# A second transposed copy of x for layer 0's residual, and a relu in two halves of PSUM banks, in a two-layer pre-activation convolution

## What is computed

```python
def _gn(v, G=8, eps=1e-5):
    # per image and group of 2 channels: (v - mean) / sqrt(var + eps)
def _conv(inputs, u, v, w, b):
    kern = jnp.einsum('lj,lk,li->ijkl', u, w, v)      # 3x3, 16 -> 16 channels
    out = lax.conv_general_dilated(inputs, kern, window_strides=(1, 1), padding='SAME', ...)
    return jax.nn.relu(out + b)
x = x + _conv(_gn(x), u0, v0, w0, b0)
x = x + _conv(_gn(x), u1, v1, w1, b1)
```

## Time and profile before

| what | value |
|---|---|
| three runs | 4683.33, 4687.26, 4693.34 us; median 4687.26 |
| the profiled execution | 4676.86 us |
| its span, first to last instruction | 4675.1 us |
| granted TensorE clock | 0.997 of full speed |
| instructions | 288889 |
| DMA | 555.71 MB, mean 119 GB/s |

### The profile page before, as it was taken

How to read it: one execution, slowest core, us unless ns; L and a number is a source line. 1 busy time by engine, 2 the same in 40 slices (tenths; PEclk the granted TensorE clock), 3 DMA queues, 4 the chain that set the end, 5 groups by cost and what they waited for, 6 DMA issues and landing times.

```text
span 4675.1 us, 288889 instructions
## 1 busy us (share of the span) xinstructions
PE 4587.9 (98%) x138240; PEld 2626.0 (56%) x138240; DVE 2845.1 (61%) x3341; ACT 2199.5 (47%) x2242; POOL 1265.0 (27%) x1093
## 2 busy tenths in 40 slices
PE   5999999999999999999999999999999999999999
PEld 3555555555555555555555555555555555555555
DVE  4656656566566566665666656656656666566564
ACT  4454444544445444444454444444544444445442
POOL 3322322323223222232232322322313223223230
PEclk9999999999999999999999999999999999999999
DMA  3333333333333333333333333333333333333323
GB/s 120 108 120 117 124 121 122 118 122 116 122 121 120 118 119 120 123 118 121 122 119 121 121 120 121 120 121 122 120 121 121 120 125 117 121 122 120 121 91 102
DMA packets 542278, 555.71 MB, mean 119 GB/s; under 512 B 16432, under 2 KB 541104, under 8 KB 541104
## 3 DMA queue, kind: packets, MB, share of 16 engines
q1 hardware_dynamic: 541104, 537.22, 35.0%
HBM read 268.72 MB, written 268.44 MB: 115 GB/s over the span
## 4 chain that ended last, share of the span: by engine, by line
PE 94%; issue 3%; ACT 1%; DVE 0%; ACTq 0%; DVEq 0%
PE ps_y L374 35%; PE ps_y L336 34%; PE ps_x L399 12%; PE ps_x L354 10%; PE ps_y L319 2%; PE ps_x L299 1%; ACT relu L457 1%; ACT relu L454 0%; PE ps_x L309 0%; DVE evens L554 0%; DVE result L571 0%; ACTq L452 0%; DVE pixels L586 0%; DVEq L100 0%; ACT evens L465 0%
## 5 line engine op out<-in xcount | busy, mean ns | idle before, releaser
L374 PE MATMUL ps_y<-odds,scaled 32*32 32x512 f32 x49152 | 1766.8, 600 | 7.9 <-issue 2.2
L336 PE MATMUL ps_y<-evens,scaled 32*32 32x512 f32 x49152 | 1745.3, 598 | 23.6 <-ACT evens L465 8.3
L574 DVE TENSOR_TENSOR odds<-ps_x,relu 128x2048 f32<-128x2048 f32 x256 | 586.8, 2292 | 1110.7 <-PE ps_x L354 842.1
L374 PEld LDWEIGHTS ps_y<-odds,scaled 32*32 32x32 f32 x49152 | 808.0, 103 | 794.2 <-issue 376.4
L336 PEld LDWEIGHTS ps_y<-evens,scaled 32*32 32x32 f32 x49152 | 852.8, 103 | 699.8 <-issue 214.0
L457 ACT ACTIVATE relu<-ps_y,bias 128x2048 f32<-128x2048 f32 x256 | 503.8, 1968 | 1094.3 <-PE ps_y L374 942.7
L280 POOL TENSOR_TENSOR fold<-fold,evens 128x1024 f32<-128x1024 f32 x384 | 845.0, 2200 | 597.3 <-DVE evens L561 309.8
L571 DVE TENSOR_TENSOR result<-ps_x,relu 128x2048 f32<-128x2048 f32 x256 | 586.6, 2292 | 636.4 <-PE ps_x L399 439.2
L454 ACT ACTIVATE relu<-ps_y,bias 128x2048 f32<-128x2048 f32 x256 | 503.7, 1968 | 920.8 <-PE ps_y L336 910.6
L354 PE MATMUL ps_x<-evens,constants 32*32 32x512 f32 x16384 | 786.7, 596 | 0.0
L399 PE MATMUL ps_x<-odds,constants 32*32 32x512 f32 x16384 | 776.2, 604 | 0.0
(11 more groups left out here) (49 smaller groups left out, 1266.7 us busy)
## 6 DMA issues: line engine op xcount, KB each, us to landing
out<-pixels SPq DMA_DIRECT2D x512, 512.0 KB, 3.5
raw<-in_x SPq DMA_DIRECT2D x256, 512.0 KB, 3.9
raw<-in_x SPq DMA_DIRECT2D x128, 576.0 KB, 4.1
raw<-in_x SPq DMA_DIRECT2D x128, 448.0 KB, 3.5
parameters<-in_params SPq DMA_DIRECT2D x2, 96.5 KB, 2.0
constants<-in_consts SPq DMA_DIRECT2D x1, 81.0 KB, 2.0
```

Source lines behind the costliest of these rows:

```text
L336: done = nc.tensor.matmul(ps_y[part, r, :], w0[rows, t * Q:(t + 1) * Q], N0[rows, k:k + EACH, i:i + HQ], start=(t == 0), stop=(t == NTAP - ...
L374: done = nc.tensor.matmul(ps_y[Q * r:Q * (r + 1), q, :], w1[p % 2][Q * q:Q * (q + 1), t * Q:(t + 1) * Q], t1[Q * q:Q * (q + 1), k:k + EACH ...
L574: nc.vector.tensor_tensor(T1[p % 2][:, EACH * f:EACH * (f + 1), 1:1 + H].rearrange("p k (r h) -> p r k h", h=HQ), ps_x[:].rearrange("p r ( ...
```

## The change

- VectorE turns x a second time, from `raw` into a new tile `N0_shifted`, one column on, that is in the pairs of `T1`. It does so in eight chunks (`turn_shifted(p, f, a)`) of the next image per image. Per image there are also three small copies into `joint`, for the pairs that cross a boundary, and one transpose of it. `SHIFTS_IN_0` and `SHIFTS_IN_1` say behind which round the chunks stand in the queue.
- The residual of layer 0 is then one product a tile with a block `same` that keeps every channel.
- The relu is two instructions of two banks each (`RELUS` = 2), in both layers. The first tap's products (`LEAD` = 1) go in the order of these halves, each half waiting for its own relu. The taps after it go over all banks in turn.
- `pixels` has four parts, used in turn, and `raw` has its own region per quarter with the column before it. SP's loads and stores stand at other places of the rounds, and a load also waits until the chunk has been turned the second time.

```diff
+RAW_Q = SLOTS * Q + ROUNDS * C
+PIXELS = 4
+SHIFTED = HALVES * ROUNDS + 4
+SHIFTS_IN_0 = (((0, 0), (0, 1)), ((1, 0),), ((1, 1),), ((2, 0),))
+SHIFTS_IN_1 = (((2, 1),), ((3, 0),), ((3, 1),), ())
...
+RELUS = 2
+BANKS = QUADS // RELUS
 HOOK_AFTER = 2
+LEAD = 1
...
+def tile_order():
+
+    lead = [(t, bank, other) for i in range(RELUS) for t in range(LEAD)
+            for other, bank in itertools.product(range(QUADS), range(BANKS * i, BANKS * (i + 1)))]
+    rest = [(t, bank, other) for t in range(LEAD, NTAP)
+            for other, bank in itertools.product(range(QUADS), range(QUADS))]
+    return lead + rest
...
+                    sp.wait_ge(shifted, shifted_by(p - 1, f, a))
...
+                ahead = C if f else 0
+                part = slice(Q * freed(f).start - ahead, Q * freed(f).stop)
+                start = raw_at(f) + C - ahead
+                sp.dma_start(raw[:, a, :, start:start + part.stop - part.start],
...
+                             pixels[:, (HALVES * f + a) % PIXELS, :].rearrange("p (q y) -> p q y", q=QUADS)
...
+                    n = round_of(0, p, 0)
+                    begun(n)
+                    load(p + 1, 3, 0)
+                    half_way(n)
+                    store(p - 2, 2, 1)
+                    begun(n + 1)
+                    load(p + 1, 3, 1)
+                    half_way(n + 1)
+                    store(p - 2, 3, 0)
...
+                    n = round_of(1, p - 1, 0)
+                    begun(n)
+                    load(p + 2, 1, 0)
+                    begun(n + 1)
+                    load(p + 2, 1, 1)
+                    half_way(n + 1)
+                    store(p - 1, 0, 0)
+                    begun(n + 2)
+                    store(p - 1, 0, 1)
...
             def conv0(p, f):
                 n = round_of(0, p, f)
-                if n:
-                    pe.wait_ge(relued, n)
...
-                for t in range(NTAP):
+                for t, r, q in tile_order():
+                    if t == 0 and q == 0 and r % BANKS == 0 and n:
+                        pe.wait_ge(relued, RELUS * (n - 1) + r // BANKS + 1)
...
+                    k = SLOTS * q + EACH * f + side
+                    rows, part = slice(Q * r, Q * (r + 1)), slice(Q * q, Q * (q + 1))
+                    done = nc.tensor.matmul(ps_y[part, r, :], w0[rows, t * Q:(t + 1) * Q],
+                                            N0[rows, k:k + EACH, i:i + HQ], start=(t == 0),
+                                            stop=(t == NTAP - 1), skip_group_check=True)
+                    last = r == QUADS - 1 and q == QUADS - 1
+                    if last and f == 0 and t == LEAD - 1:
+                        for tap in range(LEAD):
+                            wrap_pair(tap)
+                    if last and f == 0 and LEAD <= t < TAPS + 1:
...
+                    if last and t == HOOK_AFTER and f == 0:
...
-                for side in range(SIDES):
-                    for q in range(QUADS):
-                        for r in range(QUADS):
-                            k = SLOTS * q + EACH * f + side
-                            done = nc.tensor.matmul(ps_x[Q * q:Q * (q + 1), r, :], perm[Q * r:Q * (r + 1), side, :],
-                                                    N0[Q * r:Q * (r + 1), k:k + EACH, 1:1 + HQ],
-                                                    start=(side == 0), stop=(side == SIDES - 1))
+                    pe.wait_ge(shifted, SHIFTED * (p + 1))
+                for q in range(QUADS):
+                    for r in range(QUADS):
+                        done = nc.tensor.matmul(ps_x[Q * q:Q * (q + 1), r, :], same[Q * r:Q * (r + 1), :],
+                                                N0_shifted[Q * r:Q * (r + 1), q, EACH * f:EACH * (f + 1), :],
+                                                start=True, stop=True)
                 done.then_inc(x_filled, 1)
...
             def conv1(p, f):
                 n = round_of(1, p, f)
                 t1 = T1[p % 2]
-                pe.wait_ge(relued, n)
...
-                for t in range(NTAP):
+                for t, q, r in tile_order():
+                    if t == 0 and r == 0 and q % BANKS == 0:
+                        pe.wait_ge(relued, RELUS * (n - 1) + q // BANKS + 1)
...
+                    k = EACH * f + side
+                    done = nc.tensor.matmul(ps_y[Q * r:Q * (r + 1), q, :],
+                                            w1[p % 2][Q * q:Q * (q + 1), t * Q:(t + 1) * Q],
+                                            t1[Q * q:Q * (q + 1), k:k + EACH, HQ * r + i:HQ * (r + 1) + i],
+                                            start=(t == 0), stop=(t == NTAP - 1))
...
-                if y == 0:
-                    ins = nc.scalar.activation(R[:], ps_y[:], ACT.Relu, bias=bias[:, 0:1],
-                                               accum_out=acc_relu[:, f:f + 1])
-                else:
-                    ins = nc.scalar.activation(R[:], ps_y[:], ACT.Relu, bias=bias[:, 1:2])
-                ins.then_inc(relued, 1)
+                for i in range(RELUS):
+                    banks = slice(BANKS * i, BANKS * (i + 1))
+                    if y == 0:
+                        at = RELUS * f + i
+                        nc.scalar.activation(R[:, banks, :], ps_y[:, banks, :], ACT.Relu, bias=bias[:, 0:1],
+                                             accum_out=acc_relu[:, at:at + 1]).then_inc(relued, 1)
+                    else:
+                        nc.scalar.activation(R[:, banks, :], ps_y[:, banks, :], ACT.Relu,
+                                             bias=bias[:, 1:2]).then_inc(relued, 1)
...
+            def turn_shifted(p, f, a):
+                if p >= IMAGES:
+                    return
+                if p and f == 0 and a == 0:
+                    dve.wait_ge(shifted, SHIFTED * p)
+                if f == 0 and a == 0:
+                    nc.vector.tensor_copy(joint[:, :, :, C:2 * C], raw[:, :, :, C:2 * C]).then_inc(shifted, 1)
+                if p:
+                    dve.wait_ge(x_filled, round_of(0, p - 1, f) + 1)
+                turned = N0_shifted[:].rearrange("p q k (g a) -> p a q k g", a=HALVES)
+                pairs = slice(max(freed(f).start, 1), freed(f).stop)
+                start = raw_at(f) + Q * (pairs.start - freed(f).start)
+                nc.vector.transpose(turned[:, a, :, pairs, :],
+                                    raw[:, a, :, start:start + Q * (pairs.stop - pairs.start)].rearrange(
+                                        "p q (k x) -> p q k x", x=Q)).then_inc(shifted, 1)
+                if f == ROUNDS - 1 and a == 0:
+                    nc.vector.tensor_copy(joint[:, :, 1:QUADS, 0:C],
+                                          raw[:, :, 0:QUADS - 1, RAW_Q - C:RAW_Q]).then_inc(shifted, 1)
+                    nc.vector.tensor_copy(joint[:, :, 0, 0:C],
+                                          raw[:, :, QUADS - 1, RAW_Q - C:RAW_Q]).then_inc(shifted, 1)
+                if f == ROUNDS - 1 and a == 1:
+                    dve.wait_ge(shifted, SHIFTED * (p + 1) - 1)
+                    nc.vector.transpose(turned[:, :, :, 0, :], joint[:]).then_inc(shifted, 1)
+
...
-                dve.wait_ge(relued, n + 1)
+                dve.wait_ge(relued, RELUS * (n + 1))
...
+                    if ROUNDS * p + f >= PIXELS // HALVES:
+                        dve.wait_ge(image_out[a], 16 * (ROUNDS * p + f + 1 - PIXELS // HALVES))
+                    to = pixels[:, (HALVES * f + a) % PIXELS, :].rearrange("p (q k x) -> p q k x", q=QUADS, x=Q)
+                    nc.vector.transpose(to,
                                         result[:, a, :, :].rearrange("p (q k) g -> p q k g", q=QUADS)
                                         ).then_inc(turned_out, 1)
...
+            for f in range(ROUNDS):
+                for a in range(HALVES):
+                    turn_shifted(0, f, a)
...
                             turn_in(p + 1, f)
+                        for chunk in SHIFTS_IN_0[f]:
+                            turn_shifted(p + 1, *chunk)
...
                         scale_weights(0, p + 1)
                     if p:
                         turn_out(p - 1, f)
+                    for chunk in SHIFTS_IN_1[f]:
+                        turn_shifted(p + 1, *chunk)
```

More of the change, by code:

```diff
@@ L1 @@
+import itertools
 from contextlib import ExitStack
@@ L53, in turned_by, with raw_at, shifted_by @@
     return TURNS * p + (TURNS if f == ROUNDS - 1 else HALVES * (f + 1) + 1)
+def raw_at(f):
+    return Q * freed(f).start + C * f
+def shifted_by(p, f, a):
+    within = {(0, 0): 2, (3, 0): SHIFTED - 2, (3, 1): SHIFTED - 1}.get((f, a), HALVES * f + a + 2)
+    return SHIFTED * p + within
 def round_of(y, p, f):
@@ L110, in build @@
         T2 = sb("result", [P, QUADS, EACH, HQ])
-        pixels = sb("pixels", [P, HALVES, ROW])
+        pixels = sb("pixels", [P, PIXELS, QUADS * EACH * Q])
+        N0_shifted = sb("shifted", [P, QUADS, SLOTS, HQ])
+        joint = sb("joint", [P, HALVES, QUADS, 2 * C])
```

(31 more changed lines are left out.)

64 lines of the change are left out of this document (29 added, 35 removed).

## The result

The changed kernel takes 4806.03 us (median of four runs, 4804.71 to 4815.79) against 4685.85 for the kernel before in the same series: a ratio of 1.0258, 95% interval 1.0240 to 1.0276. It is slower by 120 us; the forecast was slower by 200. The granted clock is 0.997 as before.

The account below looks back on a forecast made before the run. TensorE was taken as the bound, 98% busy with 94% of the chain. Layer 0's 0.76 plus layer 1's 2.34 made 3.1 us an image, x 64 = 198, +2: 4877 from 4676.9, as median about 4887, range 4680 to 4930.

Parts of the forecast that it names:

- A: The prediction's own case, chance 0.51: longer relu intervals in both layers and late reads in layer 1, 4887 us.
- rival B: Chance 0.14: layer 1's late reads are absorbed, leaving 1.12 us an image, 4759 us.
- To take away the product alone brings nothing: Layer 0: the residual's second tap hides under a relu of the same length, so removing it is worth 0.
- The relu in halves: Relu start to second half's y: 2.35 us instead of 2.11 in layer 0, 2.16 instead of 2.02 in layer 1.
- The early half at 0.05: First tap by halves: early start gains 0.05 us a round, leaving +0.19 in layer 0, +0.09 in layer 1.
- Rival C: Chance 0.12: tiles run free, the early half counts in full, 0.54 instead of 0.05; +0.9 us an image, 4745.
- The reads late by 0.95, 1.2 and 1.56: Layer 1, f=0, f=1, f=2: shifts ahead in VectorE's queue delay small-product reads to 6.56, 5.97, 7.32 us after y's start.
- f=0 at +0.85: Layer 1, f=0: residual loads 0.95 us late, so the next y follows the residual; less 0.1, +0.85 us.
- f=2 at +1.25: Layer 1, f=2: residual loads 1.56 us late, +1.46 after 0.1 off, less 0.2 for TensorE's own stalls: +1.25 us.
- SP at 0: SP's loads and stores: same bytes in as many transfers, at 3.5 to 4 us each and 36% DMA share: 0.
- +0.15 (f=1): Layer 1, f=1: shift delays the read by 1.2 us, loads at 6.18 against 5.95; against +0.09 by the relu, +0.15.
- f=3 at +0.09: Layer 1, f=3: only the cost of the relu in halves, +0.09 us.

Follow-up runs that it names:

- e4: Kernel before with only the relu in halves and the first tap in their order: 4709.1 us, ratio 1.0061.
- e2: Changed kernel with second-turn shifts moved so the bias read (f=0) and group-sum read (f=2) come early: 4767.2 us, ratio 1.0183.
- e1: Changed kernel with the relu whole again (RELUS = 1): 4829.75 us, ratio 1.0324.
- e12: Kernel before with PSUM's halves one tap apart through the whole round, residual in two products, no second turn: 4545.5 us, ratio 0.9702.
- e9: e6 with PSUM's halves kept one tap apart through the whole round, each half signalling its own y_filled: 4542.6 us, ratio 0.9694.
- e7: e6 with the relu whole: 4761.7 us, ratio 1.0165.
- e5: Changed kernel with SP's transfers spread, one at the start and one at the middle of each round: 4788.6 us, ratio 1.0217.
- e6: Changed kernel with the edits of e5 and e2 together (transfers spread, reads early): 4729.4 us, ratio 1.0096.
- e11: Changed kernel with stores writing 8 of 128 partitions: 4755.6 us, ratio 1.0150.
- e10: Kernel before with stores writing 8 of 128 partitions: 4669.4 us, ratio 0.9970.
- e3: Changed kernel with the edits of e1 and e2 together (relu whole, reads early): 4808.3 us, ratio 1.0277.

## Why the prediction was right, and where its sizes were off

The sign held, 4806 lies in the range, and both losses that A names are there: the relus and the late reads. But they are worth some 28 (e4) and 39 us (e2), 67 of the 120, where A had 198 for them. By themselves they would give some 4753, which is rival B's number (4759), and B's mechanism, late reads absorbed, holds for much of f=0 and f=2. The other half came from stalls that had no term. That the sum ended between A and B rests on these errors against each other, which is luck; the sign does not. By its own steps:

- **"To take away the product alone brings nothing"**: right for the clean rounds of layer 0. They rose by 0.11 with half the residual, and e4, which keeps both products, has the same 8.84; with the relu whole (e1) they are at 8.73, as before. e12 and e9 agree for another order (7.97 both). Whether the missing product adds stalls elsewhere, as e7's rival has it, stays open.
- **The relu in halves**, 2.35 and 2.16 after its start: measured 2.35 and 2.17.
- **The early half at 0.05**: mis-sized. The y phase of layer 0 shortened by 0.13, so its rounds cost 0.11 and not 0.19, and layer 1's clean rounds 0.02 and not 0.09. The halves cost 26 us in all; at 4 x 0.19 + 4 x 0.09 they would have cost 72. (Rival C wanted 0.54 for the early half; the 0.13 measured is well under it.)
- **The reads late by 0.95, 1.2 and 1.56** (at 6.56, 5.97 and 7.32 after s): medians 6.35, 6.07 and 6.99. Right in kind, within 0.33.
- **f=0 at +0.85**: a quarter of it came. The period behind it rose by 0.02 clean, 0.20 at the median and 0.22 on average, where rounds of 9.6 were to show the term and 9.41 came. The prediction kept the residual's two taps at their old length from the late start. They ran from 6.62 to 8.44 (first load to last matmul start, medians), 1.82 us, where before it was 5.71 to 8.24, 2.53 us. In the lines above, 32 of its loads are out within 0.27 (2069.63); in the earlier trace rows 64 take 2.28, behind the last tap of y. That the tiles had been idle and so started together is a reading of these rows, not a test.
- **f=2 at +1.25**: +0.45 on average in the period behind it, +0.60 at the median (9.26 and 9.28, where rounds of 10.3 were to show it). The residual is compressed here too: 1.98 us from first load to last matmul start, 2.50 before.
- **SP at 0**: wrong in kind. The new order and place of the transfers cost time: e5 and e6 take 17 and 38 us away by that alone (e6 against e2), and the period ahead of f=2's relu, to which the prediction gave +0.15 (f=1), rose by 0.53. The 3.5 to 4 us a transfer of that term do not stand in the that it names.
- **f=3 at +0.09**: the period behind its relu, which holds layer 0's first y, rose by 0.32 on average, while its clean one fell by 0.07.

Term by term, each taken as the mean growth of the period behind its relu: layer 0's four rounds 0.49 where 0.76 stood, f=0 0.22 for 0.85, f=1 0.53 for 0.15, f=2 0.45 for 1.25, f=3 0.32 for 0.09. Three terms were too large by 1.70 together, two too small by 0.61. Of the 3.1 us an image forecast, 2.0 came.

The 120 us divide so: 28 are the halves (e4); 39 go when the reads are early (e2), 77 when the transfers are spread too (e6); 20 lie between e6 and e4 and are not explained. They add up to 125, as the kernel before had 4685.9 in the first series and 4681.3 in that of e4. The shares of reads and transfers depend on the order in which they are taken away.

**What the stalls are** is shown in part. TensorE's instructions come by q8 in blocks of 16 KB: 1083 of them for 276480 matmuls and loads before, 1019 for 260096 now, one for some 256 instructions. Right behind the relu of 2096.97 above stands such a stall. First its row in the changed kernel's timeline, then two lines of the same kernel's DMA view from 2095.5 to 2097 (queue: packets, MB, share):

```profile
2098.17 0.24 PEld L457 LDWEIGHTS ps_x<-odds,constants 32*32 32x32 f32 x29 [1.06 <-issue]
```

```profile
q8 instruction: 1, 0.02, 3.9%
q1 hardware_dynamic: 8, 0.01, 1.3%
```

One block starts there, at 2095.75, when a burst of loads and stores is just over (eight packets are left of it). TensorE's loads pause for 1.06 and go on at 2098.17, 2.42 after the block's start. The kernel before has the same picture: the block of the pause of the earlier trace rows starts at 2017.10, as a transfer ends, and the loads go on at 2019.46, 2.36 after it.

This holds over the whole trace. Of the pauses of over 0.6 us in y's loads that the profile puts down to "issue", the kernel before has 47, and all 47 end 2.0 to 2.8 us after the start of a block (19% of moments taken at random would). The changed kernel has 164, of which 112 end so. The count is 58 in e4, 253 in e1, 155 in e2, 152 in e5 and 128 in e6. So the change brought pauses of this kind, and e6 removed only some of them. That the blocks are held up behind data is less well borne out: 26 of the 47 and 38 of the 112 belong to a block that starts from 0.2 before to 0.5 us after the end of a burst of transfers of over 1 us, which 14% and 10% of random moments do. The gains of fewer bytes stored (e11) and of spread transfers (e5) fit it, the kernel before with thin stores (e10), still with 47 such pauses, does not. It was not tried by itself, and e11 leaves 60 us of its distance over the clean 26. Why a whole relu makes the stalls longer (e1, e3, e7) was only argued: with an early half TensorE takes eight tiles' products while the other eight still wait, and so asks for its next block sooner.

## What to carry to other kernels

Before shortening a stretch on the bounding engine, look for what else has the same length beside it: a product under a relu of equal length is worth nothing (layer 0's clean rounds take 8.84 with one product or two, e4). Then shorten the cycle itself: when a drain by another engine stands between two passes over the same banks, split the banks and keep the halves a tap apart through the whole round, not only in its first tap (7.97 against 8.84 us a round, 3% of the kernel). And count clean and mean rounds apart, because two kernels can have the same clean rounds and lie 2% apart.

## What the runs showed of the hardware

- A stretch of TensorE's products that starts after a pause was shorter than one that follows on: the residual's two taps took 1.82 us instead of 2.53 in f=0, so a start 0.9 us late cost 0.20 at the median and 0.02 in the shortest rounds.
- The halves of the relu, 1110 ns each, chain with 1.11 between their starts in layer 0 and let y's loads follow 0.15 to 0.16 after an end (2043.61 to 2043.76, behind the accumulator's read). The Trainium skill (ScalarE: Activation LUTs, What ACT_TABLE_LOAD costs) would give, as an estimate, 280 + 0.833 x 1024 = 1133 ns; the trace has 23 less.
- An order of transfers with the same bytes moved the time by 38 us of 4767 (e6 against e2), while VectorE's own waits for loads into `raw` stayed at 6 us in total (6.0 and 6.4).
- TensorE's instructions come by DMA while it runs, a block of 16 KB for some 256 of them, and in the kernel before every long pause of y's loads (47 over 0.6 us) ended 2.0 to 2.8 us after a block's start.
